# A decoder layer on one core: loads, fills and the head of the second half of the kernel placed anew

## What is computed

```python
x = x + _L0_attn_ref(_layernorm(x), ...)            # 32 heads of 32, 8 key/value heads, weights as signs
x = x + _L0_xattn_ref(_layernorm(x), pos, ctx, ...)  # the part that the change touches
x = x + _L0_ffn_ref(_layernorm(x), ...)              # one dense product and adapters of rank 32

def _L0_xattn_ref(res, ...):                         # H=256, C=4, NH=16 heads of 16
    qkv_in = rat_read(res, ...)                      # y = einsum over C, layer norm of 3 x 256
    attn_out = attention(qkv_in, qkv_w, pos)         # q, k, v products, rotation, causal softmax
    h = rat_write(res, attn_out, ...)                # h*A_full + out*B_full, A_full = exp(-delta*a)
    mlp_in = rat_read(h, ...)                        # 2 x 256
    mlp_out = silu(gate) * up                        # gate, up = mlp_in times ctx_1024, 1,024 columns
    return rat_write(h, mlp_out, ...)
```

## Time and profile before

| | busy us | share of the span |
|---|---|---|
| TensorE matmuls | 811.9 | 90% |
| VectorE | 668.6 | 74% |
| ScalarE | 450.5 | 50% |
| GpSimd | 286.5 | 32% |
| mean granted TensorE clock | | 0.926 of full |

### The profile page before, as it was taken

One profiled execution on the slowest core, in us unless ns is written; L12 is line 12 of the kernel. 1 busy time (PEld: TensorE's weight loads), 2 busy tenths in 40 slices (PEclk: granted clock), 3 DMA queues, 4 the chain that ended last, 5 costly groups with the idle time before them and its releaser, 6 DMA issues.

```text
span 905.4 us, 15537 instructions
## 1 busy us (share of the span) xinstructions
PE 811.9 (90%) x5786; PEld 424.1 (47%) x5786; DVE 668.6 (74%) x1398; ACT 450.5 (50%) x875; POOL 286.5 (32%) x289
## 2 busy tenths in 40 slices
PE   4899999999999998899977779875679999999987
PEld 3575442333333333467655323224456666656644
DVE  7875668988889885477875668536388998999861
ACT  5465528777777777023433357543244444435421
POOL 2000007677777768010010145341021212221100
PEclk8999999999999999999995588757799999999998
DMA  8676422232313141202235331101000111010011
GB/s 337 226 253 219 148 88 69 87 94 68 110 53 115 48 127 42 82 24 60 71 89 217 127 100 61 50 26 37 1 1 1 48 36 24 35 46 12 25 35 59
DMA packets 75772, 75.81 MB, mean 84 GB/s; under 512 B 37509, under 2 KB 63893, under 8 KB 75062
## 3 DMA queue, kind: packets, MB, share of 16 engines
q1 hardware_dynamic: 75142, 68.77, 24.4%
q10 hardware_dynamic: 560, 6.12, 1.7%
HBM read 53.56 MB, written 21.04 MB: 82 GB/s over the span
## 4 chain that ended last, share of the span: by engine, by line
PE 65%; DVE 17%; issue 5%; ACT 4%; SPq 3%; POOL 2%; DMA 2%; DVEq 0%; ACTq 0%; POOLq 0%; PEldq 0%
PE psum L1697 8%; PE psum L2064 6%; PE psum L1783 5%; PE psum L1834 5%; DVE m_neg L1318 4%; PE psum L1891 4%; PE psum L1823 4%; PE psum L1844 3%; PE psum L2086 3%; PE psum L1898 3%; PE psum L2025 3%; PE psum L1991 3%; PE psum L2068 3%; PE psum L1969 2%; SPq L557 2%
## 5 line engine op out<-in xcount | busy, mean ns | idle before, releaser
L1318 DVE TENSOR_REDUCE m_neg<-psum 128x1 f32<-128x512 f32 x256 | 165.5, 683 | 26.1 <-PE psum L1783 24.1
L935 ACT ACTIVATE region_x<-psum 128x512 f32<-128x512 f32 x256 | 142.6, 597 | 55.5 <-PE psum L1823 54.0
L702 POOL TENSOR_TENSOR region_p<-region_x 128x2048 f32<-128x2048 f32 x32 | 145.1, 4536 | 37.8 <-ACT region_x L935 25.0
L1783 PE MATMUL psum<-ops 96*128 96x512 f16 x256 | 96.4, 384 | 5.2 <-DVE m_neg L1318 5.1
L1823 PE MATMUL psum<-ops 98*128 98x512 f16 x256 | 95.7, 381 | 0.9 <-ACT region_x L935 0.8
L1697 PE MATMUL psum<-region_x,region_w 128*128 128x512 f16 x320 | 74.2, 388 | 1.2 <-ACT region_x L845 1.2
L1834 PE MATMUL psum<-region_x,v_g 128*32 128x512 f32 x512 | 67.8, 604 | 0.0
L1783 PEld LDWEIGHTS psum<-ops 96*128 96x128 f16 x256 | 24.8, 97 | 87.4 <-DVE m_neg L1318 68.3
L1891 PE MATMUL psum<-sign_o_all,region_a 128*128 128x512 f16 x256 | 60.2, 387 | 4.0 <-DVE region_p L1401 2.8
L2064 PE MATMUL psum<-region_a,c_o 128*128 128x512 f16 x256 | 61.0, 382 | 0.0
L1075 ACT ACTIVATE region_p<-psum 128x512 f32<-128x512 f32 (+2 forms) x96 | 39.1, 463 | 39.4 <-PE psum L1980 39.2
(11 more groups left out here) (259 smaller groups left out, 1607.5 us busy)
## 6 DMA issues: line engine op xcount, KB each, us to landing
ops<-q_scr SPq DMA_DIRECT2D x48, 128.0 KB, 2.6
region_a<-in_x SPq DMA_DIRECT2D x8, 512.0 KB, 8.3
region_a<-in_w_q SPq DMA_DIRECT2D x8, 512.0 KB, 7.5
region_w<-in_kern SPq DMA_DIRECT2D x16, 256.0 KB, 2.9
kern_scr<-region_w SPq DMA_DIRECT2D x32, 128.0 KB, 1.9
region_p<-in_x SPq DMA_DIRECT2D x8, 512.0 KB, 3.6
region_a<-kern_scr ACTq DMA_DIRECT2D x1, 4096.0 KB
out<-region_w SPq DMA_DIRECT2D x7, 512.0 KB, 2.6
```

Source lines behind the costliest of these rows:

```text
L702: pool.tensor_tensor(pair_sum[:, n], prob_a[:, 2 * n], prob_a[:, 2 * n + 1], ALU.add).then_inc(pair_ready, 1)
L935: act.activation(prob_a[:, kt, j, :], psum[:, (0, 4, 5)[(16 * i + n) % 3], :], ACT.Exp, scale=A_SCALE).then_inc(p_ready, 1)
L1318: dve.tensor_reduce(m_neg[:, i % 3, n:n + 1], psum[:, 1 + (16 * i + n) % 3, :], AX_X, ALU.max, negate=True).then_inc(s_max, 1)
L1783: pe.matmul(psum[:, 1 + (16 * i + n) % 3, :], qa_op[u][0:A_MAX, j, qt * P:(qt + 1) * P], k_op[u][0:A_MAX, :], start=True, stop=True).then_ ...
```

## The change

- `load_later` is cut in pieces. `write1` and the first half of `write2` are issued in read round 5, the second half in round 6, and `kern_scr` comes in eight pieces of 512 KB, issued by ACT behind exponential 4 and 12 of steps 3 to 6.
- In a read round `rope` of the tile before runs whole ahead of the statistics, `turn_rotated` stands right behind the read product, q, k and v are two signals (q and k, then v), q and k wait for four of the six turned parts, and the fills of rounds 6 and 7 are spread between q, k and v. In round 7 `x_turn_max(0)` comes behind v, and the copy `x_max_hi(0)` behind the copy of v.
- On SP the store of y and the maxima of a step go ahead of the wait for all stores of q and k and ahead of `load_heads`, and five small loads move from turn 0 to turn 1. The sums of the first sequence are inverted at place 2 of step 5 in place of 8, and the first y goes ahead of the maxima.
- The first tile's state is turned at place 12 of step 7 into banks 2 and 3 and its read product is made ahead of the last sums.
- Products and deltas of tile 2 go ahead of the reading of tile 1; the gate of tile 1 uses banks 4 and 5 in place of 0 and 1.

```diff
-HEAD_INVERT, ..., HEAD_DECAY = 8, 3, 6, 9, 10, 14, 2, 6
+HEAD_INVERT, ..., HEAD_DECAY, HEAD_H = 2, 3, 6, 9, 10, 14, 2, 6, 12
...
-        X_FILL = {5: ((), (), range(0, 2)), 6: (range(2, 3), range(3, 4), range(4, 10)), 7: (range(10, 11), range(11, 12), range(12, 16))}
+        X_FILL = {5: ((), (), range(0, 2), (), ()), 6: (range(2, 3), range(3, 4), range(4, 6), range(6, 7), range(7, 8)),
+                  7: (range(8, 9), range(9, 10), range(10, 12), range(12, 13), range(13, 16))}
...
             for i in range(XI):
-                if i == 1:
-                    sp.wait_ge(qk_stored, 192 * NT + 192)
-                if 1 <= i and i + 3 < XI:
-                    load_heads(i + 3)
+                if i == 5:
+                    store_inverse(0)
+                    load_y(0)
                 if i > 0:
                     store_y(i - 1)
                 if i + 1 < XI:
                     load_max(i + 1)
                 if i == 4:
                     load_sums(0)
+                if i == 1:
+                    sp.wait_ge(qk_stored, 192 * NT + 192)
+                if 1 <= i and i + 3 < XI:
+                    load_heads(i + 3)
                 if i == 5:
-                    store_inverse(0)
-                    load_y(0)
                     load_y(1)
                 if i == 0:
                     store_qk(NT - 1)
+                if i == 1:
                     sp.dma_start(read2, d["read2"]).then_inc(w2_loaded, 16)
...
-            def load_later():
+            def load_write_1():
                 act.wait_ge(op_mm, 2 * NT)
                 act.dma_start(write1, d["write1"]).then_inc(w2_loaded, 16)
-                act.dma_start(write2, d["write2"]).then_inc(w2_loaded, 16)
+            def load_write_2(h):
+                act.dma_start(write2[:, 4 * h:4 * h + 4, :], d["write2"][:, 4 * h:4 * h + 4, :]).then_inc(w2_loaded, 16)
+            def load_kern(w, q):
                 act.wait_ge(w_moved, 48 * NI)
-                act.dma_start(kern.rearrange("p w c n -> p w (c n)"), kern_scr.rearrange("w p c n -> p w (c n)")).then_inc(kern_loaded, 16)
+                act.dma_start(kern[:, w, 2 * q:2 * q + 2, :].rearrange("p c n -> p (c n)"),
+                              kern_scr[w, :, 4 * q:4 * q + 4, :].rearrange("p c n -> p (c n)")).then_inc(kern_loaded, 16)
...
                 if i + 1 < NT:
                     copy_turned(i + 1)
-                else:
-                    x_max_hi(0)
-                act.wait_ge(qkv_mm, i + 1)
+                act.wait_ge(qkv_mm, 2 * i + 2)
...
-                if i == NT - 2:
-                    load_later()
+                if i == NT - 3:
+                    load_write_1()
+                if NT - 3 <= i < NT - 1:
+                    load_write_2(i - NT + 3)
+            x_max_hi(0)
...
+                    if (i, n) == (XI - 1, HEAD_H + 2):
+                        act.wait_ge(h2T_mm, 1)
+                        turned(h2T, 2, h2T_ready)
                     if n == 8 and i + 1 < XI:
                         x_max_hi(i + 1)
+                    if 3 <= i < 7 and n % 8 == 4:
+                        load_kern((i - 3) // 2, 2 * ((i - 3) % 2) + n // 8)
...
-                    dve.wait_ge(qkv_mm, i + 1)
+                    dve.wait_ge(qkv_mm, 2 * i + 1)
...
                 if i > 0:
-                    rope(i - 1, (0,))
+                    rope(i - 1, (0, 1))
                 read_stats(i)
-                if i > 0:
-                    rope(i - 1, (1,))
                 read(i)
...
+            rope(NT - 1, (0,))
             x_max_lo(0)
-            rope(NT - 1, (0, 1))
+            rope(NT - 1, (1,))
...
+            read_2(0, 2)
             dve.wait_ge(xpv_done, 2 * XI)
             dve.sem_inc(out_stored, 16)
             to_state(1, h_in)
-            read_2(0)
...
                 mm.then_inc(y_mm, 1)
+                if i > 0:
+                    turn_rotated(i - 1)
...
-                if i > 0:
-                    turn_rotated(i - 1)
...
-                pe.wait_ge(ynT_ready, 6 * i + 6)
                 for o in range(3):
+                    pe.wait_ge(ynT_ready, 6 * i + (4 if o < 2 else 6))
...
-                mm.then_inc(qkv_mm, 1)
+                    if o > 0:
+                        mm.then_inc(qkv_mm, 1)
+                    if o < 2:
+                        x_fill(i, 3 + o)
+                if i == NT - 1:
+                    x_turn_max(0)
...
-            x_sums(XI - 1, 1)
+                    if (i, n) == (XI - 1, HEAD_H):
+                        turn_state(0, h_0, 2)
...
+            read_2(0, 2)
+            x_sums(XI - 1, 1)
+            pe.wait_ge(yT_ready, 2)
+            products_1()
+            deltas(0, 1)
             pe.wait_ge(xo_copied, XI)
-            pe.wait_ge(kern_loaded, 16 * 3)
+            turn_read(0)
+            pe.wait_ge(kern_loaded, 16 * 10)
...
-            turn_state(0, h_0)
-            pe.wait_ge(yT_ready, 2)
-            products_1()
-            read_2(0)
-            deltas(0, 1)
-            turn_read(0)
...
             read_2(1)
             deltas(1, 0)
+            pe.wait_ge(yT_ready, 3)
+            products_1()
+            deltas(0, 2)
             turn_read(1)
             for n in range(2):
-                gate_up_hi(1, 0, (n,))
-                gate_up_lo(1, 0, (n,))
-            next_products(2)
-            deltas(0, 2)
+                gate_up_hi(1, 4, (n,))
+                gate_up_lo(1, 4, (n,))
             run_rounds(pe, round_)
```

More of the change, by code:

```diff
@@ L1029, in x_copy_out, with turned @@
                 act.activation(xo_sb[i % 2], psum[:, 7, :], ACT.Copy).then_inc(xo_copied, 1)
+            def turned(to, bank, done):
+                for h in range(2):
+                    act.activation(to[:, 4 * h:4 * h + 4, :], psum[:, bank + h, :].rearrange("p (c n) -> p c n", c=4), ACT.Copy).then_inc(done, 1)
             def low_first(i):
@@ L1052, in decays @@
                 act.activation(b.abar[:, 0:3 * H], b.abar[:, 0:3 * H], ACT.Exp, scale=-1.0).then_inc(W["abar_ready"][k], 1)
-            def turned(to, bank, done):
-                for h in range(2):
-                    act.activation(to[:, 4 * h:4 * h + 4, :], psum[:, bank + h, :].rearrange("p (c n) -> p c n", c=4), ACT.Copy).then_inc(done, 1)
             def split_ctx_hi(c, h):
@@ L1109, in round_ @@
                 if first:
-                    low_first(i)
                     log_part(0, i)
@@ L1140, in round_ @@
                     gate(i, 0)
-            act.wait_ge(h2T_mm, 1)
-            turned(h2T, 6, h2T_ready)
+                if first and done != LAST:
+                    low_first(i + 1)
             low_first(1)
@@ L1153, in _ @@
             log_part(1, 0)
+            low_first(2)
             read_turned(1, y2_hi, ynT)
             decays(1, 0)
-            gate(1, 0)
+            gate(1, 4)
             run_rounds(act, round_)
```

22 lines of the change are left out of this document (10 added, 12 removed).

## The result

The changed kernel took 900.18 us (median of 20 runs, 892.87 to 904.25) beside 907.96 us for the kernel before on the same chip (20 runs, 904.17 to 919.29). The ratio is 0.9904, interval 0.988 to 0.9929: 8.7 us faster, between 6.5 and 10.9. Run again in a later group as `c1_changed` it took 897.71 us, ratio 0.9893, interval 0.9863 to 0.9923. The forecast was 897.5 us and a gain of 8.2. Runs that lie over 1.5% above the fastest of their kernel (4 of 85 of the kernel before, 3 of 6 of the one with the heads first, none of the others) are left out of all ratios and means.

What follows compares the result with a forecast made beforehand. PE bounds from 677 us on; from 456 to 677 us no engine does, only a chain of waits. 2.3 + 4.4 + 0.2 + 3.5 - 1.5 - 0.7 = 8.2 us gained, forecast 897.5 us, range 892.5 to 902.8.

Steps and rivals of the forecast that it cites:

- Part 1, the loads: Stores of tile 6, ahead of step 0: without the large load, ACT's copy of the last tile starts 1.8 us earlier.
- Part 1, the rounds: Read rounds 6 and 7: rope 0.8 us later in round 6, scores give that back, last turn 0.4 to 0.5 us earlier.
- the two scores fewer between turning and q give that back: Read round 6: two scores fewer ahead of q make up the 0.8 us by which rope is later.
- Pieces: Steps 3 to 6: eight issues on ACT lose 1.5 us, bounds 0 and 3.6; their transfers were costed at nothing.
- Part 2, SP's list: Step 2: PE's 4.04 us wait for the maxima goes; gain 4.4 us, bounds 3.0 and 5.2.
- Everything moves together, so the two add: Gains of the loads and rounds (2.3 us) and of SP's list at step 2 (4.4 us) were simply summed.
- Part 3, y of tile 0: Inverting the sums earlier gains 0.2 us; the maxima of step 6 go 0.4 us later, within 1 us of slack.
- Part 4, the state in step 7: Step 7: turning tile 0's state earlier brings its reading forward; gain 3.5 us, bounds 2.0 and 4.5.
- Part 5, products of tile 2: Between 661 and 677 us: moving them earlier gains nothing and may lower PE's clock; 0.7 us lost, bounds 0 and 3.
- A: Rival, steps 2 to 5 and the gates: PE's clock stays high, 4.6 us more gain, 893 us; chance 0.19.
- B: Rival: the stalls only move, so gains in the read rounds, step 2 and step 7 shrink; 902 us, chance 0.16.
- D: Rival, steps 3 to 6: pieces of the dense weights hold back the next maxima, 12.8 us lost, 908 us; chance 0.05.

Runs made afterwards that it cites:

- the one with the heads first: The changed kernel with SP issuing `load_heads` ahead of the store of y and the maxima in turns 2 to 4; median 900.9 us.
- loads alone: The kernel before with only the loads changed (write1 and write2 in rounds 5 and 6, dense weights in eight pieces); 904.40 us, ratio 0.9964.
- rounds alone: The kernel before with only the read rounds changed, the single load staying in round 6; 912.03 us, ratio 1.0044.

## Why the prediction was right, point by point

- **What bounds.** Right for the pair of traces: the 228 us behind `turn_state(2)` stayed (228.2 and 228.4), and all the gain between them lies ahead. But they are not fixed, as the 231.7 and 231.5 us above show.
- **Part 1, the loads** (forecast with the rounds 2.3 us; bounds 0.8 to 3.4). The stores took 7.3 us (7.5 forecast). But the copy came at 501.00, 6.9 us earlier than before (2.3 forecast, 505.6). With loads alone it came at 505.59, and step 0 started 2.3 us earlier (1.8 forecast for the loads): for the way as before, this term was sized well. What it left out is the collision that earlier rounds would meet. Put back into the changed kernel the single load costs 5.2 us at equal clock, where the forecast was 1.8 less the 1.5 of the pieces, 0.3.
- **Part 1, the rounds.** In round 6 the turn of `yn` does come 1.05 us later behind the read product (0.8 forecast). The step that failed is the next one, "the two scores fewer between turning and q give that back": round 6 became 3.3 us shorter. PE's timeline of that round, before:

```profile
474.99 1.54 PE L1898 MATMUL psum<-ident,yn 128*128 128x128 f32 x6 [0.49 <-ACT yn L1006]
...
480.25 0.95 PE L1936 MATMUL psum<-ops 48*128 48x128 f16 x2 [0.29 <-DVE m_neg L1469]
481.13 5.49 PE L1969 MATMUL psum<-region_w,ynT 128*128 128x256 f32 x12
```

  and after:

```profile
474.88 1.54 PE L1911 MATMUL psum<-ident,yn 128*128 128x128 f32 x6 [3.15 <-ACT yn L1014]
...
478.38 1.13 PE L1980 MATMUL psum<-region_w,ynT 128*128 128x256 f32 x4
...
479.71 1.13 PE L1980 MATMUL psum<-region_w,ynT 128*128 128x256 f32 x4
```

  It is four scores fewer ahead of q, not two (`range(4, 6)` for `range(4, 10)`; two of the four move in between q, k and v), by my own price of 3 us for six 2.0 us and not 1.0. q starts 3.5 us behind the turn of `yn`, 6.1 before, as PE no longer stands behind scores that wait for DVE's maxima; and the products run at 2.4 GHz, 3.4 us for the twelve in place of 5.49. In sum: 1.05 us later, 2.64 by the scores and 1.70 from q to the end of the round. I had miscounted the scores, and not asked what PE's clock would be. And the gain depends on the loads: alone the rounds gained nothing. That coupling was in the earlier trace rows to be seen (the load is issued at the end of ACT's work in round 6, so shorter rounds move it forward) and was not asked for.
- **Pieces** (1.5 us, bounds 0 and 3.6). Between nothing, at equal clock, and some 4 to 5 us, by mean times and ratios; which of the two holds is open. An issue took ACT 0.33 us, less than the 0.45 of the earlier trace rows, but the term I set to nothing, their transfers, was not nothing: the q and k of step 7, issued beside a piece, landed after 4.6 us in place of 2.4, and PE waited 1.23 us for them. The Trainium skill ("DMA: Bandwidth & Descriptors", Issuing engines are not separate DMA queues) says that transfers of different issuing engines run on the same 16 DMA engines and interleave; that row agrees, at a smaller price than the large load's.
- **Part 2, SP's list** (4.4 us, bounds 3.0 to 5.2). The stall went, and step 2 starts 18.3 us after step 0 (18 forecast, 24.0 before). Taken alone out of the changed kernel, though, it is worth 2.2 ± 1.1 us at equal clock: with loads and rounds mended, the old list makes PE wait 0.63 us, not 4.04, in a trace whose clock there was low (0.57). "Everything moves together, so the two add" is the step that was too simple. What I named as next late, the heads of step 4, cost PE 0.40 us (0.3 forecast).
- **Part 3, y of tile 0** (0.2 us). No run shows a gain; the move made SP wait for a landing ahead of the maxima of step 6, "within 1 us of slack" by my text. The slack held in most traces and not in one, where a late issue and a late landing together cost PE 5.0 us.
- **Part 4, the state in step 7** (3.5 us, bounds 2.0 to 4.5). Undone it costs 3.0 us at equal clock; in the traces the stage is shorter by 2.3 and 3.6. The chain is the one forecast: the read product ahead of the last sums, then products, deltas and the turn at 604.03, with DVE done 2 us before. The read product took 3.68 us in one trace and 2.5 in the other, for the 2.0 that I took.
- **Part 5, products of tile 2** (0.7 us lost between 661 and 677 us). There nothing was lost: 26.21 and 26.24 us, though the clock fell from 0.87 to 0.72 as feared. The 1.50 us of slack took it all; PE now turns the state with no idle time before it. 1.2 us were lost elsewhere, between readings 0 and 1, where the sixteen products of the second write took 8.17 us for 6.87 before, and undoing part 5 does not give them back. The time at equal clock points the other way from the forecast: undone, part 5 costs 0.9 us with an error of 0.7, where undoing it should have gained 0.7.
- **The sum** (8.2 us; medians 7.8, ratios 8.7 and 9.7, 10.5 at equal clock). Right, but by terms that cancel, and so in part by luck. What each part costs when it alone is undone, in us:

| part | forecast gain | at equal clock | by mean time |
|---|---|---|---|
| loads, with the pieces | 1.8 - 1.5 = 0.3 | 5.2 ± 0.6 | 3.0 |
| rounds | 0.5 | 1.2 ± 0.6 | 0.8 |
| SP's list and y of tile 0 | 4.4 + 0.2 = 4.6 | 2.2 ± 1.1 | 0.1 |
| state in step 7 | 3.5 | 3.0 ± 0.5 | 2.3 |
| products of tile 2 | -0.7 | 0.9 ± 0.7 | -0.2 |
| sum | 8.2 | 12.5 | 6.0 |

The mean times are good to 1 to 1.5 us, and by ratio no part, undone, is clearly told apart from the changed kernel (0.9874 to 0.9926, against 0.9904 and 0.9893). By both columns the loads gave more than forecast and SP's list less; the sizes are those of the yardstick.

- **Rivals.** A's extra 4.6 us did not come: the steps' clock is 0.72 for 0.71. It came in steps 0 and 1 alone (0.95 for 0.78) and was given back in steps 2 to 5 (38.1 us for 36.3). B's limits did not bind together, though part 2 by itself fell below its 3. D's mechanism is real: q and k landed late in most traces with pieces, and in one of the ten with pieces the maxima themselves landed 3.3 us late, at D's own price; on the mean it did not come near the 12.8 us that D needed.

## What to carry to other kernels

Undo each part of a change alone, and do each alone: here one half gains nothing without the other, and a part's worth depends on the others: moving the load is worth 2.4 us at equal clock in the old kernel and 5.2 beside the new rounds, and the new SP list 2.2 where its wait was 4.0 us long, since another wait stood right behind it. Where an engine's clock moves, one profile of each kernel is not enough: put the runs' times beside their mean clocks before a difference of a few us between two traces is given a cause. A load that waits for another transfer's landing belongs behind the issues that others wait for, even where it is on time in the trace at hand.

## What the runs showed of the hardware

- Runs of one kernel differ by up to 1.3% (892.87 to 904.25 us) with the same instructions, and that follows the mean granted clock, 4.45 us for 0.01. A single stretch shows how: in the trace of rounds alone the sixteen read products behind `turn_state(2)` took 3.51 us, in that of the kernel before 2.00, with the same work and the same idle stretch (1.49 and 1.50 us) ahead; the whole last stretch took 231.5 us for 228.2.
- A store issued about when a 4 MB load starts on another engine's queue can land far behind its usual time (it is some 2 us for the small transfers of the earlier trace rows): the last stores of tile 5 were issued by 482.3 us, the load at 482.15, and the buffer came free at 497.06.
